# Layer 0's first expert product: two scaled half-precision parts in each row half of the array, bias rows in place of an activation bias

## The reference, cut to what matters

```python
h = x @ Wm + bm
t = h.reshape(bs * L_ * H, HD)          # H = 8 heads, HD = 16
logits = t @ expert_emb                 # 16 experts
w = jax.nn.softmax(logits, axis=-1)
topw, topi = jax.lax.top_k(w, K)        # K = 2
hmid = jax.nn.gelu(jnp.einsum('td,edi->tei', t, W1) + b1, approximate=False)   # I = 64
eo = jnp.einsum('tei,eio->teo', hmid, W2) + b2
sel = jnp.take_along_axis(eo, topi[:, :, None], axis=1)
comb = (sel * topw[:, :, None]).sum(axis=1)
return comb.reshape(bs, L_, d) @ Wo + bo
```

## Time and profile before

| | us |
|---|---|
| median of 3 runs | 1425.36 |
| lowest and highest | 1425.2, 1428.38 |
| span of the profiled execution | 1426.4 |
| TensorE busy in it | 1370.7 |
| VectorE busy | 1205.4 |
| ScalarE busy | 1101.6 |
| GpSimd busy | 283.0 |

### The profile page before, as it was taken

How to read it: one execution, slowest core, us unless ns; L and a number is a source line. 1 busy time by engine, 2 the same in 40 slices (tenths; PEclk the granted TensorE clock), 3 DMA queues, 4 the chain that set the end, 5 groups by cost and what they waited for, 6 DMA issues and landing times.

```text
span 1426.4 us, 25921 instructions
## 1 busy us (share of the span) xinstructions
PE 1370.7 (96%) x9689; PEld 675.9 (47%) x9689; DVE 1205.4 (85%) x2663; ACT 1101.6 (77%) x2071; POOL 283.0 (20%) x239
## 2 busy tenths in 40 slices
PE   5999999999989998999999999999999999999998
PEld 4552332322258885333343333443333345566796
DVE  6898876785389979999999999888888869999997
ACT  4678989899957724888878888888888877887545
POOL 5210010000033321111211011111011113234452
PEclk9999999999999999999999999999999999999999
DMA  4238788767610001000000000000000000000000
GB/s 113 41 92 173 159 193 190 170 134 170 147 57 1 1 1 75 1 1 1 1 1 1 1 1 1 2 1 1 1 2 1 1 30 1 1 9 8 9 16 23
DMA packets 29949, 65.38 MB, mean 46 GB/s; under 512 B 5376, under 2 KB 16896, under 8 KB 28544
## 3 DMA queue, kind: packets, MB, share of 16 engines
q1 hardware_dynamic: 29824, 63.72, 19.0%
HBM read 54.27 MB, written 9.44 MB: 45 GB/s over the span
## 4 chain that ended last, share of the span: by engine, by line
PE 67%; DVE 17%; DMA 5%; POOL 4%; ACT 2%; issue 2%; SPq 1%; DVEq 0%; ACTq 0%; POOLq 0%
PE ps L2028 16%; PE ps L2018 12%; PE ps L516 6%; PE ps L525 6%; PE ps L1997 6%; PE ps L2041 4%; DVE p6ac L2555 3%; PE ps L2008 3%; DMA p1GB<-gscr 2%; PE ps L534 2%; POOL WA L2235 1%; PE ps L2490 1%; POOL WA L2239 1%; DVE st L164 1%; DMA p1R<-tscr 1%
## 5 line engine op out<-in xcount | busy, mean ns | idle before, releaser
L2137 ACT ACTIVATE p4E<-ps,p4mx,p4sc 128x512 f32<-128x512 f32 x512 | 393.4, 778 | 62.6 <-DVE p4mx L2090 60.8
L2085 DVE TENSOR_REDUCE p4mx<-ps 128x2 f32<-128x1024 f32 x205 | 249.7, 1218 | 29.2 <-PE ps L2018 28.1
L2028 PE MATMUL ps<-p4E,p4vn 128*64 128x512 f32 x1024 | 243.0, 599 | 0.2
L2018 PE MATMUL ps<-p4T 64*128 64x512 f16 x1536 | 199.3, 379 | 3.8 <-ACT p4E L2137 3.5
L2160 POOL TENSOR_TENSOR p4vn<-p4v,p4zs 128x512 f32<-128x512 f32 x64 | 66.7, 1042 | 503.4 <-DVE p4zs L2093 469.6
L657 DVE SCALAR_TENSOR_TENSOR p1Pb<-ps,WB,p1GB 128x512 f32<-128x512 f32 x128 | 95.4, 748 | 64.9 <-PE ps L525 55.0
L752 ACT ACTIVATE p1g<-ps,WB 128x1024 f32<-128x1024 f32 x128 | 135.4, 1121 | 12.6 <-PE ps L516 6.6
L516 PE MATMUL ps<-p1R,p1w1s 128*128 128x512 bf16 x512 | 134.0, 381 | 6.4 <-DMA p1R<-tscr 5.3
L2018 PEld LDWEIGHTS ps<-p4T 64*128 64x128 f16 x1536 | 58.3, 94 | 157.1 <-ACT p4E L2137 86.0
L525 PE MATMUL ps<-p1g,WB 128*32 128x512 f32 x512 | 129.1, 601 | 2.9 <-DVE p1Pb L657 2.7
L525 PE MATMUL ps<-xn,WB 128*32 128x512 f32 x256 | 128.3, 602 | 0.2
(11 more groups left out here) (374 smaller groups left out, 2586.0 us busy)
## 6 DMA issues: line engine op xcount, KB each, us to landing
p1GB<-gscr SPq DMA_DIRECT2D x64, 512.0 KB, 7.5
p1R<-tscr SPq DMA_DIRECT2D x64, 128.0 KB, 6.2
gscr<-p1gT SPq DMA_DIRECT2D x16, 256.0 KB, 6.8
tscr<-p1tp SPq DMA_DIRECT2D x24, 128.0 KB
WB<-in_w SPq DMA_DIRECT2D x1, 2560.0 KB, 9.1
X<-in_x SPq DMA_DIRECT2D x8, 256.0 KB, 5.7
out<-X SPq DMA_DIRECT2D x7, 256.0 KB, 2.3
WA<-in_w SPq DMA_DIRECT2D x4, 438.5 KB, 8.6
```

What stands on the lines that cost most here:

```text
L2018: y = p.e.matmul(ps[:, banks[hh], :], t[rows, q, 128 * j:128 * j + 128], t[rows, 2 + r, :], start=o == 0, stop=o == 2)
L2028: t = p.e.matmul(ps[64 * hh:64 * hh + 64, self.bank["ctx", n], :], vn[n % 2][:, j, 64 * hh:64 * hh + 64], E[2 * (n % 2) + hh][:, j, :], st ...
L2085: v.e.tensor_reduce(m, ps[:, low:low + 2, :], AX, ALU.max).then_inc(v.own.h, v.one())
L2137: a.e.activation(self.E[2 * i + hh][:, j, :], ps[:, banks[hh], :], ACT.Exp, bias=self.mx[i][:, j, hh:hh + 1], scale=pre.sc[:, 1, 0:1], acc ...
```

## The change

Each of h and W1 is scaled by powers of two and split into two half-precision parts instead of three bfloat16 ones. One row half of the array (64 partitions) now holds, for one head, h's high part twice, its low part once (16 rows each) and rows of 2^13 whose weights are b1's two parts; the other half holds the other head of the pair. The product is therefore two matmuls of 64 rows, one in each row half, with the weights present in both halves. The gelu has a scale (a column of `sw`) in the place of its bias.

```diff
-                p.wait_ge(k.sem("R", b % 2), 128 * (b // 2 + 1))
+                p.wait_ge(k.sem("R", b % 2), 64 * (b // 2 + 1))
                 for hh in range(2):
-                    t = p.e.matmul(ps[:, ka + hh, :], self.w1s[:, 128 * ep:128 * ep + 128], self.R[b % 2][:, 2 * hp + hh, :], start=True, stop=True)
+                    at = slice(64 * hh, 64 * hh + 64)
+                    t = p.e.matmul(ps[:, ka + hh, :], self.w1s[at, 128 * ep:128 * ep + 128], self.R[b % 2][at, hp, :], start=True, stop=True)
 
...
-                               bias=k.Wt(1, "b1")[:, ep:ep + 1]).then_inc(k.sem("gelu").h, 1)
+                               scale=self.sw[:, 5:6]).then_inc(k.sem("gelu").h, 1)
...
-                hT, tp = self.hT[x % 2], self.tp[x % 2]
                 v.wait_ge(k.sem("hT"), x + 1)
-                v.wait_ge(k.sem("tp"), 3 * x)
-                v.wait_ge(k.sem("ts", x % 2), 48 * (x // 2))
-                v.e.tensor_copy(tp[0][:, :], hT[:, :]).then_inc(k.sem("tp").h, 1)
-                v.wait_ge(k.sem("tp"), 3 * x + 1)
-                v.e.tensor_tensor(self.tr[:, :], hT[:, :], tp[0][:, :], ALU.subtract).then_inc(k.sem("tr").h, 1)
+                v.wait_ge(k.sem("ts", x % 2), 32 * (x // 2))
+                v.e.tensor_scalar(self.tp[x % 2][0][:, :], self.hT[x % 2][:, :], self.sw[:, 0:1], None, ALU.mult).then_inc(k.sem("tp").h, 1)
             elif what == "parts 1":
                 tp = self.tp[x % 2]
-                v.wait_ge(k.sem("tr"), x + 1)
-                v.e.tensor_copy(tp[1][:, :], self.tr[:, :]).then_inc(k.sem("tp").h, 1)
-                v.wait_ge(k.sem("tp"), 3 * x + 2)
-                v.e.tensor_tensor(tp[2][:, :], self.tr[:, :], tp[1][:, :], ALU.subtract).then_inc(k.sem("tp").h, 1)
+                v.wait_ge(k.sem("tp"), 2 * x + 1)
+                v.e.scalar_tensor_tensor(tp[1][:, :], self.hT[x % 2][:, :], self.sw[:, 0:1], tp[0][:, :], ALU.mult, ALU.subtract).then_inc(k.sem("tp").h, 1)
...
                 i = x % 2
-                sp.wait_ge(k.sem("R", i), 128 * (x // 2))
-                for j in range(3):
-                    sp.wait_ge(k.sem("tp"), 3 * x + j + 1)
-                    sp.e.dma_start(self.tscr[i][j].rearrange("j h n -> h j n"), self.tp[i][j][:, :]).then_inc(k.sem("ts", i).h, 16)
+                sp.wait_ge(k.sem("R", i), 64 * (x // 2))
+                for j in range(2):
+                    sp.wait_ge(k.sem("tp"), 2 * x + j + 1)
+                    sp.e.dma_start(self.tscr[i][j].rearrange("e j a n -> a e j n"), self.tp[i][j][:, :]).then_inc(k.sem("ts", i).h, 16)
             elif what == "parts in":
                 i = x % 2
-                sp.wait_ge(k.sem("ts", i), 48 * (x // 2 + 1))
+                sp.wait_ge(k.sem("ts", i), 32 * (x // 2 + 1))
                 sp.wait_ge(k.sem("mm1"), 32 * (x - 1))
-                if x == 1:
-                    sp.wait_ge(k.sem("w1parts"), 1)
-                for g, j in enumerate((0, 0, 0, 1, 1, 1, 2, 2)):
-                    sp.e.dma_start(self.R[i][16 * g:16 * g + 16, :, :], self.tscr[i][j]).then_inc(k.sem("R", i).h, 16)
+                sp.wait_ge(k.sem(("nth", "ones0")[i]), 3)
+                for e in range(2):
+                    for j, at, n in ((0, 0, 2), (1, 32, 1)):
+                        src = self.tscr[i][j, e].rearrange("j a n -> j (a n)").unsqueeze(0).to_broadcast([n, 16, 2048])
+                        sp.e.dma_start(self.R[i][64 * e + at:64 * e + at + 16 * n, :, :].rearrange("p a n -> p (a n)"), src).then_inc(k.sem("R", i).h, 16)
...
+    def fill(self, e, i, sem):
+
+        for r in (32, 96):
+            e.e.memset(self.R[i][r:r + 32, :, :], 2.0 ** 13).then_inc(self.k.sem(sem).h, 1)
+
```

```diff
+        v.wait_ge(k.sem("w1sum"), 1)
+        v.e.tensor_scalar(nb[:, :], k.ps[:, 6, 0:4], 2.0, 2.0 ** -80, ALU.mult, ALU.max).then_inc(v.own.h, v.one())
+        v.wait_ge(v.own, v.n)
+        v.e.scalar_tensor_tensor(nb[:, 1:2], nb[:, 0:1], 128.0, nb[:, 1:2], ALU.mult, ALU.add).then_inc(k.sem("nb1").h, 1)
...
+        v.e.tensor_scalar(w1z[:, :], w1f, sw[:, 3:4], None, ALU.mult).then_inc(v.own.h, v.one())
+        t = v.n
+        yield
+        v.wait_ge(v.own, t)
+        v.e.scalar_tensor_tensor(w1s[:, :], w1f, sw[:, 1:2], w1z[:, :], ALU.mult, ALU.subtract).then_inc(k.sem("w1parts").h, 1)
```

More of the change, by code:

```diff
@@ L255 @@
         "gpsimd": (
[L256 removed]
+            "tttt6t6t6t6t66655y?E5E5E5F555EFFEEFEFEFFZF"),
         "sync": (
@@ L308, in steps @@
         every |= {f"rank {i}": blocks for i in range(11)}
-        every |= {what: range(1) for what in ("mean", "gram out", "cov", "wt", "moments", "coef 0", "coef 1", "next stats", "next rows", "next turn")}
+        every |= {what: range(1) for what in ("mean", "gram out", "cov", "wt", "moments", "coef 0", "coef 1", "next stats", "next rows", "next turn", "bound")}
         every |= {"exp": range(5), "sum": range(1, NB), "w1": range(4), "load": [2] + [(4, i) for i in range(W4PARTS)], "parts out": blocks, "parts in": blocks, "gates": units, "mm1": range(256), "gelu": range(256)}
@@ L377, in evacuated @@
             p.wait_ge(k.sem("x1"), x + 1)
+    def fill(self, e, i, sem):
+        for r in (32, 96):
+            e.e.memset(self.R[i][r:r + 32, :, :], 2.0 ** 13).then_inc(self.k.sem(sem).h, 1)
     def weights(self, v):
[L380 to L383, removed]
+        k, q, nb, sw, half = self.k, self.q, self.nb, self.sw, self.k.C("half3")
+        w1f, w1s, w1z = k.Wt(1, "w1"), self.w1s, self.w1z
@@ L390, in weights @@
+        v.wait_ge(v.own, v.n)
+        v.e.tensor_tensor(q[:, 2:3], q[:, 2:3], half[:, 1:2], ALU.mult).then_inc(v.own.h, v.one())
+        v.e.tensor_copy(q[:, 1:2], k.Wt(1, "bm")).then_inc(v.own.h, v.one())
+        v.wait_ge(v.own, v.n)
+        v.e.tensor_tensor(q[:, :], q[:, :], q[:, :], ALU.mult).then_inc(k.sem("w1sq").h, 1)
         yield
-        v.wait_ge(v.own, t2)
-        v.e.tensor_copy(w1p[1], w1r).then_inc(v.own.h, v.one())
+        v.wait_ge(k.sem("w1sum"), 1)
+        v.e.tensor_scalar(nb[:, :], k.ps[:, 6, 0:4], 2.0, 2.0 ** -80, ALU.mult, ALU.max).then_inc(v.own.h, v.one())
@@ L398, in weights @@
         v.wait_ge(v.own, v.n)
-        v.e.scalar_tensor_tensor(w1s[:, :], w1p[1], p3[:, 1:2], w1s[:, :], ALU.mult, ALU.add).then_inc(v.own.h, v.one())
-        t6 = v.n
+        v.e.reciprocal(nb[:, 0:1], nb[:, 1:2]).then_inc(v.own.h, v.one())
+        v.e.tensor_scalar(sw[:, 0:1], nb[:, 1:2], 2.0 ** 13, None, ALU.mult).then_inc(v.own.h, v.one())
+        v.e.scalar_tensor_tensor(sw[:, 1:2], half[:, 2:3], nb[:, 1:2], half[:, 1:2], ALU.mult, ALU.add).then_inc(v.own.h, v.one())
+        v.wait_ge(v.own, v.n)
@@ new lines, in weights @@
+        v.e.scalar_tensor_tensor(sw[:, 2:3], nb[:, 3:4], nb[:, 0:1], nb[:, 2:3], ALU.mult, ALU.min).then_inc(v.own.h, v.one())
+        v.wait_ge(v.own, v.n)
+        v.e.tensor_scalar(sw[:, 2:3], sw[:, 2:3], 2.0 ** 13, None, ALU.mult).then_inc(v.own.h, v.one())
+        v.wait_ge(v.own, v.n)
+        v.e.tensor_tensor(sw[:, 1:2], sw[:, 1:2], sw[:, 2:3], ALU.mult).then_inc(v.own.h, v.one())
+        v.e.tensor_tensor(sw[:, 4:5], sw[:, 0:1], sw[:, 2:3], ALU.mult).then_inc(v.own.h, v.one())
+        v.wait_ge(v.own, v.n)
@@ L401, in weights @@
+        v.e.tensor_tensor(sw[:, 3:4], sw[:, 1:2], half[:, 0:1], ALU.mult).then_inc(v.own.h, v.one())
+        v.e.reciprocal(sw[:, 5:6], sw[:, 4:5]).then_inc(v.own.h, v.one())
+        v.wait_ge(v.own, v.n)
+        v.e.tensor_scalar(w1z[:, :], w1f, sw[:, 3:4], None, ALU.mult).then_inc(v.own.h, v.one())
+        t = v.n
         yield
-        v.wait_ge(v.own, max(t4, t6))
-        v.e.scalar_tensor_tensor(w1s[:, :], w1r, p3[:, 2:3], w1s[:, :], ALU.mult, ALU.add).then_inc(k.sem("w1parts").h, 1)
+        v.wait_ge(v.own, t)
@@ L442, in tensor @@
                 t.then_inc(k.sem("moments").h, 1)
+            elif what == "bound":
+                p.wait_ge(k.sem("ones0"), 1)
+                p.wait_ge(k.sem("w1sq"), 1)
+                p.e.matmul(ps[:, 6, 0:4], self.on[:, :], self.q[:, :], start=True, stop=True).then_inc(k.sem("w1sum").h, 1)
             elif what == "proj":
@@ L775, in gpsimd @@
                 g.e.tensor_tensor(sc[:, 1, :], sc[:, 0, :], k.C("mhalf")[:, 0:3], ALU.pow).then_inc(k.sem("bnrstd").h, 1)
+            elif what == "bound":
+                g.wait_ge(k.sem("nb1"), 1)
+                g.e.tensor_tensor(self.nb[:, 1:4], self.nb[:, 1:4], k.C("mhalf")[:, 0:3], ALU.pow).then_inc(k.sem("nbr1").h, 1)
             elif what == "stats":
@@ L2840, in _constants @@
     red[p, 32 + 16 + p % 16] = 1
-    part = np.array([0, 1, 2, 0, 1, 2, 0, 1])[p // 16]
+    row = p % 64
+    lows, bias = (row // 16 == 1) | (row == 49), (row == 48) | (row == 49)
     return _pack("c", {
@@ L2845, in _constants @@
         "tokid": p[:, None] + 128.0 * np.arange(32)[None, :],
-        "part3": (part[:, None] == np.arange(3)[None, :]), "mhalf": np.full((128, 64), -0.5),
+        "half3": np.stack([lows, row < 48, bias], 1), "mhalf": np.full((128, 64), -0.5),
```

53 lines of the change are left out of this document (31 added, 22 removed), and 3 rows, old and new, of tables (AGAIN, KINDS).

## The result

The changed kernel takes 1419.2 us at the median of 5 runs (1415.9 to 1422.5), beside 1425.4 us for the kernel before, also of 5. The ratio is 0.995, with a 95% interval of 0.9934 to 0.996. It is faster, as forecast, but by 6 us where 28.5 us were forecast, and the time lies outside the predicted range (1388 to 1412). The profiled span is 1417.4 us, 9.0 us less than before. Two numbers split that: the last gelu now starts at 379.84 us where it started at 390.63, 10.8 us earlier, and the rest of the span is 1.8 us longer (1037.6 for 1035.8). The forecast had the last gelu at 362.1 us. So 17.7 us are missing inside the stretch that the change touches.

A forecast was written before the change was run, and what follows sets the result against it. TensorE was taken to bound the first-layer stretch, ScalarE's 253 us floor after the change; with 7 us of loss 260 us, 25.5 us less. Plus 3 us at the start: 1425.4 - 28.5 = 1397 us, range 1388 to 1412.

The forecast's parts named there:

- The price of a pair: First-layer products: two 64-row matmuls in different row halves run at once, 0.215 us a pair, saving 51.8 us of TensorE work.
- a change of split: TensorE in the first-layer stretch: each change costs 0.10 us; 200 changes become 247, adding 4.7 us.
- rival 2: TensorE in the stretch: every change of split costs a matmul's tail, 0.17 us; 1404 us, chance 0.06.
- rivals 2, 3 and 4: The fourth: TensorE's halves run one after the other and every change drains; 22 us more, less 3, 1444 us, chance 0.04.
- rival 3: TensorE's halves do not overlap in the first-layer products; 1427 us, chance 0.03.
- the three signs that the prediction named for being wrong: Pairs over 0.3 us, TensorE waiting over 20 us for `gated`, or the last gelu later than 372 us.
- rival 1: VectorE and the two shared banks become the pace, TensorE's waits doubling to 28 us; 1407 us, chance 0.19.
- The start: Before the first `mm1`, which waits for `R`: the load lands sooner, 2.6 to 3.3 us gained, 3 taken.
- The scales: VectorE's scale instructions ahead of block 0's q k: no time lost, done at 39.7 us, -0.9 to +1.6 us.
- ScalarE's floor: First-layer stretch: gelus at 1.00 us each plus exponentials and table loads need 253 us; ScalarE becomes the bound.
- Parts, DMAs and VectorE in this stretch: First-layer stretch: fewer instructions, DMAs and bytes; `gated`'s 6.7 us wait for gates should shrink, counted as no gain.
- the 7 us that I took for the coupling of TensorE and ScalarE: ScalarE's loss to late TensorE products above 253 us: between none and 13.9 us, half taken.

The follow-up runs named there:

- Run 1: The changed kernel with both matmuls of each product in the lower row half, so that the pair cannot overlap: 1431.9 us.
- run 6: The changed kernel with seven gate loads moved ahead in SyncE's queue and both matmuls of each product in the lower row half: 1428.5 us.
- run 10: The changed kernel with seven gate loads moved ahead in SyncE's queue, and each gelu at 512 columns instead of 1024: 1389.5 us.
- run 11: The kernel before, with each gelu at half its width: 1427.2 us, 0.999 of before.
- run 5: The kernel before, with the same seven gate loads moved ahead in SyncE's queue as in run 4: 1425.1 us, 0.998 of before.
- run 4: The changed kernel with seven gate loads moved ahead of the parts' steps in SyncE's queue, same bytes: 1407.4 us.
- run 2: The changed kernel with gate loads of half the size, the first head's gates serving both heads: 1408.0 us.
- run 3: The kernel before, with the same halved gate loads as in run 2: 1424.2 us, 0.998 of before.
- run 7: Run 4's kernel with VectorE's second part of block 1 moved 17 letters earlier: 1408.4 us.
- run 9: Run 7's kernel with block 1's parts written out ahead of a gate load instead of behind it: 1404.9 us.
- Run 8: Run 7's kernel with gate loads of half the size, the first head's gates serving both: 1406.1 us.

## Why the prediction was right in sign and wrong in size

**The price of a pair** (0.215 us) and **of a change of split** (0.10 us, also beside the full-height split that layer 2 never showed) were right to the digits of the trace; rivals 2, 3 and 4 fall with them. Run 1 is rival 3 made real, and takes 1431.9 us where the rival gave 1427; run 6, with the loads in time, takes 1428.5. The rule of the Trainium skill, TensorEngine Tiling (Array Packing), section Key Properties, that a change of mode drains the array, would stand for a drain of 0.10 us here and not for the 0.17 of rival 2. Of the three signs that the prediction named for being wrong, the last gelu later than 372 us came; the one on `gated` is taken up with rival 1 below.

**The start** was right but for its size: 3.85 us against 3, which is 0.55 us beyond its upper bound of 3.3. The scales cost nothing. The memsets were not quite covered at first: the first rows' statistics begin at 5.38 us for 4.56, and by the coefficients of block 0 (35.28 us for 35.04) two thirds of that are made up.

**ScalarE's floor** of 1.00 us a gelu was right, and so was the statement that ScalarE becomes the bound, once the loads are in time. Runs 10 and 11 show it: half the gelu takes 17.9 us off the changed kernel with its loads in time, and none off the kernel before. The Trainium skill, on the same page, section Performance Considerations (PSUM Bottleneck), says that tiling speeds up TensorE but not the evacuation of PSUM, whose copy may become the bottleneck after a fourfold speedup. Here it was the bound after a twofold speedup of `mm1` alone; run 10 agrees, with its 17.9 us.

**The step that failed** is the one in the paragraph *Parts, DMAs and VectorE in this stretch*: "the 6.7 us that `gated` waits for gates lie behind such reads and should shrink". I took fewer bytes of `R` ahead of a load as a shorter wait for it. The wait grew from 6.7 to 13.5 us, for the same three loads. Two things add up. The loads take longer to land behind the changed parts and reads (10.0, 12.4 and 11.1 us for 9.0, 8.1 and 8.2), at TensorE's old cost too (run 1); why they do stays open. And VectorE comes for them sooner than it does in run 1, whose reads are the same and whose pace is the old one. The queue's order, which issues these loads 7 to 11 us after their buffers are free, is old: to put it right is worth 0.2% in the kernel before (run 5) and 11.8 us here (run 4, which moves letters alone). Halving the loads alone wins 11.3 us here (run 2) and 0.2% before (run 3).

Each wait is now on the path, which the old trace could not show: `gated` is late, `comb`'s bank is not free, `mm1` behind it in TensorE's string is late, and ScalarE runs on only for the gelus whose banks are already full. After TensorE's stop at 213.40 us that is 2.6 us, and TensorE stands 3.7. From 215 to 220 us the granted clock is 0.59, near the lower of its levels of 1.2 and 2.4 GHz. That the slow clock adds to the loss was read and not tested.

**The second miss** is block 1's `R`, 3.1 to 3.6 us of wait that the prediction did not name, since before, that load was 2.0 us late and hidden among TensorE's other waits. Runs 7 and 9 differ by the place of one letter, by 2.9 us in the last gelu and by 3.6 us in the median; they ran on two chips and their intervals overlap, so what this wait costs is likely but not shown.

**The third** is the 7 us that I took for the coupling of TensorE and ScalarE. Run 8 has no late load. Its gelu of step 15 starts at 102.40 us and its last at 367.53, 265 us for a floor of 253: 12 us. The upper bound, 13.9 us, would have been the better choice.

The 17.7 us missing at the last gelu are then: 9.8 us for the order of the gate loads (379.84 to 370.08, run 4), 2.1 us for block 1's `R` (to 367.96, run 9), and the 5.9 us that are left, from 362.1 to 367.96, mostly for the coupling. These are differences of single profiles; the first is clear of noise, the other two are not. Another 1.8 us came behind the last gelu; run 4 has 1.6 of them back (1036.0 us from there to the end), for a reason that I didn't look for.

Rival 1 gave 1407 us, which is what runs 2 and 4 measure, but by a mechanism that the traces do not show: weight loads for `comb` waited 9.8 us for `gated`, not 28, and less than the 11.7 of the earlier trace rows. Over all rows in which TensorE waits for `gated`, from 100 to 395 us, it is 19.9 us before and 29.2 us in the changed kernel, so that the sign of over 20 us came by this count; run 4, with the loads in time, is back at 19.9. It was the late loads, not VectorE's own pace.

## What to carry to other kernels

When a change relieves the bound engine, take every wait for a load that the old trace shows on another engine, even one that costs nothing there, and price it as if it lay on the path: here 6.7 us of such waits, worth 0.2% before, became 13.5 us and some 11 us of the time. Fewer bytes in the queue are no reason that a load lands sooner; take the time from issue to landing and to first use. Look for loads whose buffer has been free for microseconds and which stand behind something that waits for a landing: a few letters moved were worth 11.8 us, about what the overlap of the matmuls was with the old order. And a relief is worth what the next floor leaves: 51.8 us of TensorE work became some 20 us at best, because ScalarE's floor stood 32 us under the stretch and the two engines still wait for each other.

## What the runs showed of the hardware that I had not expected

- A gate load of 512 KB lands 6.6 us after issue at the median (7.5 before the change), and 12.4 us after it at unit 25, behind four reads of `R`, with the DMA engines' share down to 0.12 before the loads issued with it had landed. A 256 KB one takes 3.4 us. The write of the parts took 7.4 us (run 7) and 8.9 us (run 9) beside gate loads, and 3.0 us where none was under way.
- The change of split costs 0.10 us whatever stands beside the half-height product: 128x32 or 128x128, both in the first timeline above.
- TensorE's granted clock was 0.59 from 215 to 220 us, behind a stop of 3.7 us, and 0.50 from 124 to 126 us behind the stop at the load of unit 6; around the third stop, of 2.6 us, it stayed at 1.00 (268 to 276 us). Before, the stretch had a mean of 1.00.
